# A decoder layer on one core: the order of the loads and transposes in its first body, and twelve matmuls more

## The reference

```
x = x + self_attention(layernorm(x))         # 16 heads of 32, 4 key/value heads, ALiBi, only pairs outside a window
x = x + cross_attention(layernorm(x), ctx)   # 32 heads of 16, 8 key/value heads, ctx (8, 256, 128) is key and value
x = x + ffn(layernorm(x))                    # 32 experts, 4 of them per token by a gate, and a shared expert
```

```
q = (x * cw) @ Wq;  k, v = split(x @ Wkv)
attn = softmax(where(allowed, -1e9, q k^T / sqrt(32) - slope * |i - j|))
out = (attn v) @ Wo + bo
```

## Time and profile before

| | |
|---|---|
| three runs | 1028.26 us median, 1026.06 to 1032.23 |
| profiled execution | 1033.69 us, its span 1031.9 us |
| mean granted clock of TensorE | 0.944 |
| busy share of the span | PE 89%, DVE 55%, ACT 34%, POOL 32% |
| body 0 | to about 95 us |

### The profile page before, as it was taken

The page is one execution under the profiler, slowest core; times in us unless marked ns, Lnnn a source line. Parts: engine busy times, 40 slices in busy tenths (PEclk is TensorE's granted clock), DMA queues, the critical chain, the costliest instruction groups (busy, mean ns, idle before and its releaser), DMA issues.

```text
span 1031.9 us, 16245 instructions
## 1 busy us (share of the span) xinstructions
PE 913.8 (89%) x6168; PEld 555.8 (54%) x6168; DVE 567.6 (55%) x1284; ACT 347.4 (34%) x699; POOL 328.7 (32%) x322
## 2 busy tenths in 40 slices
PE   5457899899999999999999999989999899998980
PEld 4335545654864764674674575364677444444440
DVE  1234855886785785796688677575352122222220
ACT  4031046246336325416425524516300122222210
POOL 4001000220530351242152053033314155555774
PEclk9568679999999999999999999989999999999995
DMA  4812301400410510340240230081433599999652
GB/s 140 292 41 71 73 3 48 118 3 26 126 36 2 133 35 2 83 125 3 79 106 24 67 99 2 20 289 42 133 113 93 170 327 328 336 332 308 137 65 32
DMA packets 101920, 115.14 MB, mean 112 GB/s; under 512 B 12482, under 2 KB 80352, under 8 KB 101840
## 3 DMA queue, kind: packets, MB, share of 16 engines
q1 hardware_dynamic: 83908, 94.42, 29.7%
q0 software_dynamic: 14480, 16.55, 8.2%
q10 hardware_dynamic: 3456, 3.15, 1.2%
HBM read 70.90 MB, written 16.88 MB: 85 GB/s over the span
## 4 chain that ended last, share of the span: by engine, by line
PE 55%; DMA 16%; DVE 12%; issue 6%; ACT 5%; SPq 2%; POOL 2%; ACTq 0%; POOLq 0%; DVEq 0%
DMA out<-arena,half_ids 8%; PE qa L1483 6%; PE qx L1421 5%; PE vb L1432 5%; DVE mxx L1028 4%; DMA out<-res,half_ids 4%; PE qa L1279 4%; PE pt L1197 4%; ACT arena L637 4%; PE qa L1197 3%; PE qx L1365 3%; PE qa L1615 3%; DMA qs<-arena 2%; SPq L365 2%; PE qa L1313 2%
## 5 line engine op out<-in xcount | busy, mean ns | idle before, releaser
L1028 DVE TENSOR_REDUCE mxx<-qx 128x2 f32<-128x512 f32 x256 | 168.2, 686 | 43.5 <-PE qx L1365 40.2
L637 ACT ACTIVATE arena<-qx 128x512 f32<-128x512 f32 x256 | 146.2, 601 | 128.6 <-PE qx L1421 107.8
L637 ACT ACTIVATE arena<-qa 128x512 f32<-128x512 f32 (+2 forms) x125 | 67.4, 540 | 214.8 <-PE qa L1615 100.2
L491 POOL TENSOR_TENSOR rstd<-mv,power 128x2 f32<-128x2 f32 x24 | 17.2, 718 | 376.3 <-DVE mv L864 376.3
L1615 PE MATMUL qa<-arena 128*128 128x512 f32 x256 | 116.9, 600 | 1.1 <-ACT arena L637 1.1
L1365 PE MATMUL qx<-arena 96*128 96x256 bf16 x512 | 102.9, 290 | 14.1 <-DVE mxx L1028 9.7
L1421 PE MATMUL qx<-arena 98*128 98x512 bf16 x256 | 94.8, 392 | 6.9 <-ACT arena L637 2.9
L624 POOL DMA_INDIRECT out<-arena,half_ids x44 | 68.6, 1559 | 59.9 <-DMA out<-arena,half_ids 26.9
L1432 PE MATMUL vb<-arena 128*32 128x256 f32 x1024 | 82.5, 394 | 1.6 <-ACT arena L637 0.4
L1365 PEld LDWEIGHTS qx<-arena 96*128 96x128 bf16 x512 | 46.3, 101 | 57.5 <-DVE mxx L1028 26.3
L1155 DVE SCALAR_TENSOR_TENSOR arena<-arena,qa 128x256 f32<-128x256 f32 x32 | 13.5, 422 | 111.6 <-ACT arena L637 108.3
(11 more groups left out here) (201 smaller groups left out, 1580.2 us busy)
## 6 DMA issues: line engine op xcount, KB each, us to landing
arena<-in_L_ffn_w SPq DMA_DIRECT2D x96, 512.0 KB
qs<-arena SPq DMA_DIRECT2D x24, 384.0 KB
arena<-arena SPq DMA_DIRECT2D x72, 128.0 KB, 3.3
res<-in_x SPq DMA_DIRECT2D x8, 512.0 KB, 8.2
xnd<-arena SPq DMA_DIRECT2D x8, 512.0 KB
ks<-arena SPq DMA_DIRECT2D x48, 64.0 KB, 2.0
arena<-arena SPq DMA_DIRECT2D x48, 64.0 KB
arena<-arena ACTq DMA_DIRECT2D x24, 128.0 KB, 3.5
```

Of the source, the lines that this page charges most:

```text
L637: nc.scalar.activation(dst, src, func, **kw).then_inc(s[signal], 1)
L1028: v_.reduce_max(mxx[:, col:col + 3:2], xbank[v % 2].rearrange("p (h n) -> p h n", h=2), AX.X).then_inc(s["x_max"], 1)
```

## The change

Five edits, all in body 0 alone but for the order of SP's waits in the second:

- `later_loads` is called after the two shift rows instead of after the query rows. The tokens of batch 1 are loaded second, with a semaphore `x1_in` of their own, which DVE waits for in body 0; it waits for the others in body 1.
- SP waits for `q_hi` before each of the two transfers of `qh` and for `q_split` before that of `ql` (in every body; in the others POOL still makes `ql`).
- In body 0 the two subtractions of POOL (`ql`, and the context's third part) are made by DVE.
- TensorE transposes `xn1` of batch 1 before `xn2`, and waits for `ln2_stats` ahead of it, since `qa` holds the projection until DVE has read it.
- `keep_busy(n)` issues n matmuls of the identity by the query weights, 128x512 in f32, into the bank `xbank[0]`, which nobody reads in body 0: four ahead of the self scores, five after the transposes of the maxima, three between the two sets of transposes.

```
 def later_loads():
-    for dst, src in ((wo_s, wo), (gw_s[:], gw)):
-        go(dst, src.rearrange("(c p) n -> p c n", p=P), "w_in")
-    for b in range(1, RING):
+    go(wo_s, wo.rearrange("(c p) n -> p c n", p=P), "w_in")
+    go(tokens(1), rows[:, 2:4], "x1_in")
+    go(gw_s[:], gw.rearrange("(c p) n -> p c n", p=P), "w_in")
+    for b in range(2, RING):
         go(tokens(b), rows[:, 2 * b:2 * b + 2], "x_in")
...
-    hold(sp, s["q_split"], k + 1)
-    for m, part in enumerate((qh, qh, ql)):
+    for m, part, signal in ((0, qh, "q_hi"), (1, qh, "q_hi"), (2, ql, "q_split")):
+        hold(sp, s[signal], k + 1)
         go(qs[m:SPLIT_ROWS:3].bitcast(F32), part.bitcast(F32), "qs_in")
-    if k == 0:
-        later_loads()
...
     go(qs[101:102].bitcast(F32), nml[:].bitcast(F32), "shift_in")
+    if k == 0:
+        later_loads()
...
 # GpSimd
-if a:
+if a and x:
     pool.wait_ge(s["q_hi"], k + 1)
     nc.gpsimd.tensor_tensor(ql, qf, qh.bitcast(F32), ALU.subtract).then_inc(s["q_split"], 1)
...
-    if a and v == AT_CONTEXT + 6:
+    if a and x and v == AT_CONTEXT + 6:
...
 # VectorE, body 0
 queries()
+dve.wait_ge(s["q_hi"], k + 1)
+v_.tensor_tensor(ql, qf, qh.bitcast(F32), ALU.subtract).then_inc(s["q_split"], 1)
 context_rem()
+dve.wait_ge(s["c_mid"], k + 1)
+v_.tensor_tensor(kp[2], kr, kp[1], ALU.subtract).then_inc(s["c_split"], 1)
...
 if k == 0:
-    dve.wait_ge(s["x_in"], RING * 16)
+    dve.wait_ge(s["x1_in"], 16)
+if k == 1:
+    dve.wait_ge(s["x_in"], RING * 16 - 16)
...
 # TensorE
+def keep_busy(count):
+    for _ in range(count):
+        mm(xbank[0], ident[:], wq_s[:, 0, :], start=True, stop=True)
...
 if a and not x:
+    keep_busy(4)
     for u in range(AU):
         self_scores(u)
     self_maxima()
+    keep_busy(5)
...
 elif a:
+    pe.wait_ge(s["xn1"], k + 2)
+    pe.wait_ge(s["ln2_stats"], k + 1)
+    transpose_norm(xn1, qa, "x_t")
+    keep_busy(3)
     pe.wait_ge(s["xn2"], k + 1)
     transpose_norm(xn2, pt, "n_t")
-    pe.wait_ge(s["xn1"], k + 2)
-    transpose_norm(xn1, qa, "x_t")
```

More of the change, by code:

```diff
@@ L260, in build @@
         xo_bank = [va[:, :], va[:, :], pt[:, :]]
-        names = """mats_in const_in ident_ready const_moved const_ready clear x_in wkv_in wq_in w_in shared_in ctx_in
+        names = """mats_in const_in ident_ready const_moved const_ready clear x_in x1_in wkv_in wq_in w_in shared_in ctx_in
             ln1_stats ln2_stats ln3_stats ln1_rstd ln2_rstd ln3_rstd ln1_shift ln3_shift xn1 xn2 xn3 abs_sum diag x_t xt_ready cw_t
```

## The result

The changed kernel takes 1013.75 us at the median of six runs (1010.07 to 1017.52), the kernel before 1027.18 (1024.74 to 1032.23): a ratio of 0.9859, 95% interval 0.9837 to 0.9881. The gain is 13.4 us. Forecast were 8.4 and a range down to 1014.5, so the sign is right and the size is wrong.

A forecast was written before the change was run, and what follows sets the result against it. The first body was taken as a single chain between engines, with TensorE stopping three times and its clock falling. Terms -1.8 - 1.5 - 5.2 + 0.3 - 1.5 - 0.4 + 1.7 = -8.4 us took 1028.26 to 1019.9, range 1014.5 to 1026.0.

The forecast's parts named there:

- The query rows: Body 0, before the self scores: VectorE's 0.96 us subtraction and issue by thirds start the last third earlier, -1.8 us.
- the 1.5 of all bodies: Bodies 1 to 7, before the self scores: the last query third starts 1.2 us sooner; -1.5 us, mostly in body 1.
- The bulk loads: Body 0, maxima to keyed scores: with the loads behind them, shift rows land 2.7 us after ready, not 7.9; -5.2 us.
- the rival of a long landing: Body 0's shift rows: landing stays near 6 us for another reason, 4.0 of the 5.2 go, 1023.9; chance 0.03.
- The twelve matmuls: TensorE's stops from body 0's start to the second norm's transposes: four, five and three fillers, 0.47 us each at full clock.
- the rival of the kept clock: Body 0: the clock is kept through the first stop, self scores about 4 us shorter, 1015.9; chance 0.08.
- The term that I put at 0: Body 0's self scores: they stay at half clock despite the four matmuls ahead of them, gain 0.
- The keyed stage: Body 0, keyed scores to first division: the five matmuls bring the clock back sooner, -1.5 us, bounds 0 and 2.5.
- The third stop: Body 0, before the second norm's transposes: three matmuls may keep the clock or delay; -0.4 us, bounds -1.0 and +0.6.
- The order of the transposes: Between body 0's projection and body 1's queries: turning the order by itself gains nothing, as ScalarE's token-weight scaling is late.
- The new stop: Before body 1's query matmuls: TensorE waits up to 3 us for ScalarE and loses the clock, +1.7 us.
- bodies from 2 on that differ by over 1 us: Sign of being wrong: bodies from 2 on shorter or longer by over 1 us.

The follow-up runs named there:

- loads_alone: The kernel before with only the bulk loads moved behind the first shift rows, with the batch 1 tokens' own wait: 1019.35 us, ratio 0.9904.
- no_four: The changed kernel without the four matmuls ahead of the self scores: 1019.41 us, ratio 0.9936.
- two_for_four: The changed kernel with two matmuls in place of four ahead of the self scores: 1024.71 us, ratio 0.9920.
- no_twelve: The changed kernel without any of the twelve added matmuls: 1017.90 us, ratio 0.9908.
- no_five: The changed kernel without the five matmuls after the maxima: 1017.56 us, ratio 0.9927.
- no_three: The changed kernel without the three matmuls between the two sets of transposes: 1015.79 us, ratio 0.9904.
- five_for_four: The changed kernel with five matmuls in place of four ahead of the self scores and nothing else: 1015.99 us, ratio 0.9873.
- best_again: Repeat: the changed kernel with five matmuls ahead of the scores, none between the transposes, GpSimd's body 1 bias addition later: 1010.55 us, ratio 0.9838.
- second group: Runs on chip 6: one part alone on the kernel before, and the changed kernel with later query rows held; kernel before there 1028.0 us.
- third group: Runs on chip 10: the changed kernel with transpose order, number of added matmuls or GpSimd's bias addition varied; kernel before there 1032.5 us.
- twelve_alone: The kernel before with only the twelve matmuls added, transposes in the old order: 1025.86 us, ratio 0.9969.

## Why the prediction was wrong, point by point

**The query rows.** -1.96 for -1.8: right, and so is VectorE's 0.96 us for the subtraction. For the 1.5 of all bodies, the stage before the self scores of body 1 went down from 11.20 us by 0.75 (by 1.1 and 1.3 in other profiled executions); from body 2 on nothing shows.

**The bulk loads.** -5.42 for -5.2, shown alone by loads_alone. The landing is 2.0 us, so the loads ahead made it long, and the rival of a long landing falls. Whether they did so by their place in the queue or by the bandwidth that they took, no run tells apart. The page "DMA: Bandwidth & Descriptors" of the Trainium skill advises, in "Rules for kernel authors", to issue early; the measurement decides against it here, where a 12 KB transfer on the path came behind 6.9 MB and took 5.96 us to land instead of 2.0. The tokens of batch 1 came 0.76 us late and cost nothing.

**The twelve matmuls: the step that failed.** "One takes 0.47" at full clock. I took the x of a row for the number of matmuls: x16 for the projection, x8 for the values. The code has eight there (two tiles by four chunks), not the sixteen that I named in describing the kernel before, and four here, and the 32 query matmuls are sixteen; the trace gives each of these f32 matmuls two records. So one added matmul takes 0.9 us at full clock (four in 3.60), double what I priced, and by the same count twice 0.83 at half. The argument that over 3 us of standing still remain came from that price, and with it the rival of the kept clock had only 0.08. In truth the four run to 32.9 when the clock falls under them, and the stop left is 1.5 us. The term that I put at 0 measured 3.5 us, in five of the eight profiled executions. no_four gives it back whole, and two_for_four, which takes the 1.9 us that I had priced for four, shows what I forecast: 10.5 us. In the other three of the eight the forecast of a stop over 3 us and of lost scores came true by luck: four at full clock end at 31.2 to 32.0, about where I had four at half clock end.

The same error had a second side that I also missed: where the clock is lost in the scores and the five are there, the keyed scores start 6.0 to 7.4 us after the maxima (six profiled executions). no_twelve, with lost scores and no five, has 4.74, so the five delay them by 1.2 to 2.7 us. I had allowed 0.5.

**The keyed stage.** -1.93 for -1.5, shown by no_five: right. The five delay nothing here only because the clock is already full when they begin.

**The third stop.** +0.35 for -0.4, inside its bounds of -1.0 and +0.6; the three overshoot by 1.3 us. no_three shows them to be worth nothing in these stages.

**The order of the transposes.** "Turning the order by itself gains nothing" was wrong by 0.7 us in the profiled pair, and the stretch is 0.3 to 2.5 us shorter over all profiled executions. I read one execution in which keys and values just ended with ScalarE's result (7.01 and 7.04 us after the split), so I saw neither that keys and values can be the later ones nor that ScalarE's result can come sooner. In the pair it is the second: ScalarE's three issues take 2.14 us instead of 2.81. That the order makes them shorter is not shown.

**The new stop.** It is there, 2.55 us, and the clock fell: +1.68 for +1.7. But of the thirteen profiled executions with the new order only four (the changed kernel's first, two_for_four, five_for_four and best_again) lost it; nine have 6.77 or 6.78 us. As a mean over executions the term is nearer 0.5 (an estimate: four of thirteen times 1.7).

**What I did not count.** The projection takes 8.5 to 8.8 or 9.9 to 10.1 us by where in it the clock comes back, in kernels of either kind. And the profiled kernel before had 82.3 to 83.1 us from one body's maxima to the next from body 3 on, where all kernels run on chips 8, 6 and 7 have 81.0 to 81.5, the changed one among them; on chip 10 all four kernels, variants of the changed one, have the longer ones. That is 5.0 of the 7.5 us between the two spans; another 4.1 lie behind the last maxima, a part that varies from 399 to 407 us among kernels with the same code there; and -1.7 in body 2, which varies from 80.7 to 83.0. One place of the 5.0 us, in the weighing matmuls behind the maxima of body 5, first in the kernel before and then in the changed one:

```profile
470.79 0.91 PE L1478 MATMUL va<-arena,ones 128*32 128x128 f32 x6
472.00 0.38 PE L1478 MATMUL va<-arena,ones 128*32 128x128 f32 x2 [0.30 <-issue]
```

```profile
456.47 0.40 PE L1492 MATMUL va<-arena,ones 128*32 128x128 f32 x8
```

A pause in the middle of these matmuls, with nothing that released it: the group lasts 1.5 us instead of 0.3. The 5.0 us are about what the profiled execution stood above the median, 5.4, and I had put that down to the clock. What the pause is stays open. The prediction had named bodies from 2 on that differ by over 1 us as a sign of being wrong; they did in the profiled pair. Since variants of the kernel before have the short bodies (second group) and variants of the changed one the long ones (third group), it is not the change that makes them.

The sum: 13.4 us by the medians against 8.4 forecast, and 13.4 in the profiled pair up to the maxima of body 1. Of the 5.0 us between them, 3.5 are the self scores in the pair; the rest is the clock in the projection (1.2) and the stretch before the queries (0.7), less 0.4 by which the other terms together fell short. That the medians divide in the same way is not shown. The range missed by 0.75 us because its low end took in only a part of that rival.

## What to carry to other kernels

Count the instructions in the code before you divide a row of the trace by its x: each of these f32 matmuls has two records here, while an f32 transpose by the identity has one (eight in `transpose_norm`, x8 in the trace). Filler for a stop must be priced at both levels of the clock, since a filler that fits at half clock leaves a gap at full, and one that fits at full overruns at half; both happened in one kernel. A small transfer on the critical path should be issued ahead of bulk that has time, and two profiled executions should be compared over the stages that the change does not touch before their spans are compared.

## What was not expected of the hardware

- TensorE busy for 9.73 of 10.40 us with the self scores never left half clock, in any of the eight profiled executions in which they began there.
- Eight profiled executions of the same four matmuls, with the same landing behind them, show that the clock falling under them (5.3 us) went with full clock in the scores, and full clock under them (3.6 us) with its loss, without exception. With the landing 2 us later (twelve_alone) 5.3 us did not save it.
- Five matmuls of 4.46 us and a stop of 2.3 us behind them left the scores at full clock in one execution (6.97 us) and lost it in another (9.35).
- VectorE's 128x512 norm instruction takes 1.56 us with GpSimd's addition beside it and 0.66 without (3.12 and 1.31 for two).
